# A vision tower with attention and a mixture of experts: scores from one projection, norms on ScalarE, a new order of TensorE's work per step

## The reference

```python
z = _layernorm(patches, ln1_g, ln1_b)
z = jnp.einsum('bnp,pe->bne', z, W_proj) + b_proj
z = _layernorm(z, ln2_g, ln2_b)
z = jnp.concatenate([cls, z], axis=1) + pos_emb
```

```python
q = jnp.einsum('blh,oh->blo', x, Wq) + bq
k = jnp.einsum('blh,oh->blo', x, Wk) + bk
v = jnp.einsum('blh,oh->blo', x, Wv) + bv
attn = jnp.einsum('blh,bmh->blm', q / hidden, k)
attn = jnp.where(eye[None, :, :], mask_value, attn)
return jnp.einsum('blm,bmh->blh', jax.nn.softmax(attn, axis=-1), v)
```

## Time and profile before

| | |
|---|---|
| median of 3 runs | 497.82 us (497.40 to 695.03) |
| the profiled execution | 497.69 us, of which span 496.0 us |
| PE busy | 376.4 us, 76% |
| DVE busy | 330.7 us, 67% |
| ACT busy | 210.0 us, 42% |
| POOL busy | 239.3 us, 48% |
| mean granted clock of TensorE | 0.861 of full |

### The profile page before, as it was taken

The page is one execution under the profiler, slowest core; times in us unless marked ns, Lnnn a source line. Parts: engine busy times, 40 slices in busy tenths (PEclk is TensorE's granted clock), DMA queues, the critical chain, the costliest instruction groups (busy, mean ns, idle before and its releaser), DMA issues.

```text
span 496.0 us, 7921 instructions
## 1 busy us (share of the span) xinstructions
PE 376.4 (76%) x2309; PEld 333.4 (67%) x2309; DVE 330.7 (67%) x863; ACT 210.0 (42%) x466; POOL 239.3 (48%) x399
## 2 busy tenths in 40 slices
PE   4585999999999998430136799999999999992000
PEld 1485999999999997330023599999999999991000
DVE  6463688777787866788881366667666676740692
ACT  4222445445445443272000256565656556532241
POOL 3254777777777755300002600835537274044395
PEclk9779899999999998755555699999999999997555
DMA  6423123323323201290002323656546475132833
GB/s 188 108 85 104 45 76 103 91 74 109 86 78 109 65 28 58 74 152 1 0 22 83 92 86 106 150 156 165 114 130 138 151 173 134 17 39 28 212 92 105
DMA packets 44676, 47.42 MB, mean 96 GB/s; under 512 B 11851, under 2 KB 36550, under 8 KB 44646
## 3 DMA queue, kind: packets, MB, share of 16 engines
q1 hardware_dynamic: 37940, 38.91, 28.0%
q0 software_dynamic: 5632, 7.36, 9.1%
q10 hardware_dynamic: 1074, 0.79, 0.6%
HBM read 32.38 MB, written 14.67 MB: 95 GB/s over the span
## 4 chain that ended last, share of the span: by engine, by line
PE 69%; DVE 12%; POOL 6%; DMA 4%; SPq 3%; issue 2%; ACT 1%; ACTq 0%; POOLq 0%; DVEq 0%
PE pz L796 16%; PE pall L809 16%; PE pall L703 9%; PE pall L672 8%; DVE wproj L1071 5%; PE pall L679 3%; SPq L423 3%; PE pall L769 2%; PE pall L713 2%; PE pz L659 2%; POOL stage L1354 2%; PE pall L720 1%; PE pall L821 1%; DMA stage<-in_x 1%; PE pall L692 1%
## 5 line engine op out<-in xcount | busy, mean ns | idle before, releaser
L1325 POOL DMA_INDIRECT y_rows<-rows,didx x32 | 50.7, 1585 | 95.2 <-ACT rows L606 87.9
L796 PE MATMUL pz<-halves 128*128 128x448 f32 x384 | 90.6, 373 | 2.1 <-DVE halves L1153 2.1
L809 PE MATMUL pall<-halves 128*128 128x448 f32 x384 | 89.9, 369 | 0.6 <-DVE halves L1148 0.6
L796 PEld LDWEIGHTS pz<-halves 128*128 128x128 f32 x384 | 73.7, 192 | 8.8 <-DVE halves L1153 2.5
L809 PEld LDWEIGHTS pall<-halves 128*128 128x128 f32 x384 | 70.9, 188 | 6.8 <-DVE halves L1148 1.0
L590 ACT ACTIVATE wproj<-pz,b1t 128x448 f32<-128x448 f32 x64 | 40.6, 635 | 73.8 <-PE pz L796 70.3
L1315 POOL DMA_INDIRECT rows<-x_rows,gidx x32 | 34.6, 1082 | 69.6 <-DVE gidx L1133 60.0
L703 PE MATMUL pall<-halves 128*112 128x256 f32 x396 | 55.1, 296 | 9.0 <-DVE halves L981 9.0
L1146 DVE CAST halves<-wproj 128x448 fp32r<-128x448 f32 x64 | 26.6, 416 | 50.0 <-ACT wproj L590 46.0
L703 PEld LDWEIGHTS pall<-halves 128*112 128x112 f32 x396 | 50.8, 186 | 9.9 <-DVE halves L981 7.4
L1223 POOL TENSOR_TENSOR rs<-rs,neghalf 112x1 f32<-112x1 f32 x88 | 50.1, 570 | 7.3
(11 more groups left out here) (211 smaller groups left out, 736.3 us busy)
## 6 DMA issues: line engine op xcount, KB each, us to landing
stage<-in_w SPq DMA_DIRECT2D x32, 512.0 KB, 4.2
stage<-in_x SPq DMA_DIRECT2D x64, 108.0 KB
x_rows<-x SPq DMA_DIRECT2D x22, 224.0 KB, 3.3
y_rows<-zero SPq DMA_DIRECT2D x22, 112.0 KB
stage<-y_rows SPq DMA_DIRECT2D x3, 448.0 KB, 5.4
out<-stage SPq DMA_DIRECT2D x7, 192.0 KB
scratch<-y_rows SPq DMA_DIRECT2D x2, 448.0 KB, 8.5
wproj<-in_w_proj ACTq DMA_DIRECT2D x1, 768.0 KB
```

What stands on the lines that cost most here:

```text
L796: m = nc.tensor.matmul(bank(k % 2)[:, 0:SLOTS], w[:, c, k * 128:(k + 1) * 128], xs[:, e % 2, c, :], start=(n == 0), stop=(n == 3 * EC - 1))
L809: m = nc.tensor.matmul(pall[:, 2 * (e % 2) + o, 0:SLOTS], w[:, k, o * 128:(o + 1) * 128], hs[:, k % 2, :], start=(k == 0 and n == 0), stop ...
L1325: pool.indirect_dma_start(y_rows, bass.IndirectOffsetOnAxis(ap=didx[:, k:k + 1], axis=0), y[:, e % 2, j, :], None, compute_op=ALU.add).the ...
```

## The change

**Scores from one projection.** The scores of a tile are x1 Wq' Wk x1' plus terms of the biases. Once, in steps 0 and 1, PE transposes both weights and multiplies them to one 256x256 matrix (`wqk`, kept in the place of `wq`), and makes the vectors that the biases give. Per tile there is then one projection t = x1 Wqk + tb (4 matmuls in place of 8), and the scores are t times x1's own transposes. The part of the bias that belongs to the key row rides as a 257th column of the value projection, from which DVE makes the exponential's offset (two small instructions, L1080 and L1083, in place of one).

**Norms on ScalarE.** ACT scales the projected row (L558), and writes x1 (L593) and x2 (L533); DVE did these three. DVE multiplies by the second norm's weights as it subtracts the mean (L1058). POOL now makes an offset as third small instruction for these two norms as well (`scaled`), and no longer multiplies. ACT also copies the logits (L562); the router's bias is added to all tiles at once later. POOL's addition of `lnb` moves into the experts, three tiles behind each gather.

**Four x slots**, loaded four tiles ahead, with one buffer for the normalised x in place of two.

The core of the diff:

```diff
-        wv = sb("wv", [128, EC, ED])
+        wqk = wq
+        wv = sb("wv", [128, EC, ED + 1])
...
-        xin = stage[0:P, 0:2 * PD].rearrange("p (s f) -> p s f", s=2)
-        xn = stage[0:P, 2 * PD:4 * PD].rearrange("p (s f) -> p s f", s=2)
+        xin = stage[0:P, 0:4 * PD].rearrange("p (s f) -> p s f", s=4)
+        xn = stage[0:P, 4 * PD:5 * PD]
...
+            for t in range(2, 4):
+                sp.wait_ge(s_xz, t + 1)
+                load_x(t, t)
+
+            def step(i, slot):
+                par = slot % 2
+                t = i + 4
                 if live(t):
                     need(sp, x_n, i + 1)
-                    load_x(t, par)
+                    load_x(t, slot)
...
+                t = i - 4
+                if live(t):
+                    plain(act, (x2T_ps, t - 1), (x2_out[par], 16 * (t // 2) if isinstance(t, int) else (t - par) * 8),
+                          (g_nb, t + 1))
+                    nc.scalar.activation(x2[:, par, :], tile_of(H, t), ACT.Identity, bias=rs[:, 3, 2:3],
+                                         scale=rs[:, 3, 1:2]).then_inc(x2_ok, 1)
+                t = i + 1
+                if live(t):
+                    high_x(t)
                 t = i - 3
+                if live(t):
+                    need(act, pT_ps, t + 1)
+                    need(act, o_ps, t)
+                    nc.scalar.copy(probT[:, :], bank(5)[0:P, 128:128 + P]).then_inc(pT_sb, 1)
...
+                t = i - 2
+                if live(t):
+                    need(act, t_ps, t + 1)
+                    need(act, s_ps, t)
+                    for c in range(EC):
+                        a = nc.scalar.activation(tT[:, c, :], bank(3)[:, c * P:(c + 1) * P], ACT.Identity,
+                                                 bias=tb[:, c:c + 1])
+                    a.then_inc(t_sb, 1)
+                t = i
+                if live(t):
+                    plain(act, (z_2, t + 1), (z_rs, t + 1))
+                    nc.scalar.activation(tile_of(H, t), z2[:, :], ACT.Copy, scale=rs[:, 1, 1:2]).then_inc(z_sc, 1)
+                t = i - 5
+                if live(t):
+                    plain(act, (l_ps, t + 1))
+                    nc.scalar.copy(LG[:, :, at(t)] if not isinstance(t, int) else LG[:, :, t:t + 1],
+                                   bank(2)[0:P, 256:256 + E].rearrange("p (e a) -> p e a", a=1)).then_inc(l_sb, 1)
...
+                t = i - 1
+                if live(t):
+                    need(act, x1T_ps, t + 1)
+                    need(act, s_ps, t - 1)
+                    nc.scalar.copy(x1T[:, odd, :], bank(6)[:, 0:EC * P]).then_inc(x1T_sb, 1)
+                t = i - 4
+                if live(t):
+                    need(act, x2T_ps, t + 1)
+                    need(act, l_ps, t)
+                    nc.scalar.copy(x2T[:, :], bank(3)[:, 256:256 + EC * P]).then_inc(x2T_sb, 1)
+                t = i - 2
                 if live(t):
                     need(act, s_nmx, t + 1)
                     need(act, pT_ps, t)
+                    need(act, g_h, t - 1)
                     nc.scalar.activation(prob[:, :], masked[:, :], ACT.Exp, bias=nmax[:, 0:1], scale=1.0 / ED,
+                                         accum_out=psumr[:, par:par + 1]).then_inc(p_ok, 1)
+                t = i + 2
+                if live(t):
+                    norm_x(t, (slot + 2) % 4)
                 t = i
                 if live(t):
+                    plain(act, (x1T_ps, t - 1), (h_nb, t + 1))
+                    nc.scalar.activation(x1[:, par, :], tile_of(H, t), ACT.Identity, bias=rs[:, 2, 2:3],
+                                         scale=rs[:, 2, 1:2]).then_inc(x1_ok, 1)
...
+                if isinstance(i, int) and i == 1:
+                    pe.wait_ge(c_ws, 2)
+                    pe.wait_ge(c_bq, 1)
+                    for o in range(EC):
+                        for c in range(EC):
+                            nc.tensor.matmul(bank(3)[:, o * ED:(o + 1) * ED], wqs[:, c, o * 128:(o + 1) * 128],
+                                             wks[:, c, :], start=(c == 0), stop=(c == EC - 1))
+                    for o in range(EC):
+                        for k, w in enumerate((wks, wqs)):
+                            for c in range(EC):
+                                nc.tensor.matmul(bank(4)[:, k * EC + o:k * EC + o + 1], w[:, c, o * 128:(o + 1) * 128],
+                                                 bqk[:, k * EC + c:k * EC + c + 1], start=(c == 0), stop=(c == EC - 1))
+                    for c in range(EC):
+                        m = nc.tensor.matmul(bank(4)[0:P, 2 * EC:2 * EC + 1], bqrep[:, c, :], bqk[:, EC + c:EC + c + 1],
+                                             start=(c == 0), stop=(c == EC - 1))
+                    m.then_inc(c_qk, 1)
                 t = i - 2
                 if live(t):
+                    if isinstance(t, int) and t == 0:
+                        pe.wait_ge(c_tv, 4)
+                    need(pe, x1T_sb, t + 1)
+                    need(pe, t_sb, t)
+                    need(pe, x2T_sb, t - 2)
+                    xt_ = x1T[:, par, :].rearrange("p (c r) -> p c r", c=EC)
+                    for o in range(EC):
+                        for c in range(EC):
+                            m = nc.tensor.matmul(bank(3)[:, o * P:(o + 1) * P], wqk[:, c, o * 128:(o + 1) * 128],
+                                                 xt_[:, c, :], start=(c == 0), stop=(c == EC - 1))
+                    m.then_inc(t_ps, 1)
+                t = i - 5
+                if live(t):
+                    need(pe, x2T_sb, t + 1)
+                    need(pe, l_sb, t)
+                    need(pe, z_2, i + 1 if not isinstance(i, int) else min(i + 1, TILES))
                     for c in range(EC):
+                        m = nc.tensor.matmul(bank(2)[0:P, 256:256 + E], x2T[:, c * P:(c + 1) * P], rw[:, c, :],
                                              start=(c == 0), stop=(c == EC - 1))
+                    m.then_inc(l_ps, 1)
...
+                t = i - 2
+                if live(t):
+                    need(pe, t_sb, t + 1)
+                    need(pe, s_msk, t)
+                    need(pe, pT_sb, t)
+                    for c in range(EC):
+                        m = nc.tensor.matmul(bank(5)[0:P, 0:P], tT[:, c, :], xt_[:, c, :],
+                                             start=(c == 0), stop=(c == EC - 1))
+                    m.then_inc(s_ps, 1)
...
+                    need(dve, z_ps, t + 1)
+                    need(dve, z_2, t)
+                    V_.bn_stats(zstat[:, :], bank(2)[0:P, 0:ED]).then_inc(z_st, 1)
+                    plain(dve, (z_st, t + 1), (z_rs0, t))
+                    V_.bn_aggr(zmv[:, :], zstat[:, :]).then_inc(z_mv, 1)
                     if isinstance(t, int) and t == 0:
+                        dve.wait_ge(c_g, N_G)
+                        V_.tensor_tensor(posb[:, :], posb[:, :], posadd[:, :], ALU.add).then_inc(c_dve, 1)
+                    plain(dve, (z_mv, t + 1), (z_sc, t))
+                    V_.scalar_tensor_tensor(z2[:, :], bank(2)[0:P, 0:ED], zmv[:, 0:1], g2m[:, :],
+                                            ALU.subtract, ALU.mult).then_inc(z_2, 1)
...
+                    V_.tensor_scalar(nm0[:, :], smax[:, :], v[:, par, ED:ED + 1], -1.0 / ED, ALU.add, ALU.mult)\
+                        .then_inc(s_nm0, 1)
+                    need(dve, s_nm0, t + 1)
+                    V_.scalar_tensor_tensor(nmax[:, :], v[:, par, ED:ED + 1], 1.0 / ED, nm0[:, :],
+                                            ALU.mult, ALU.add).then_inc(s_nmx, 1)
...
+            def scaled(slot, mv, ready, n, mid, done, nb):
+
+                rstd(slot, mv, ready, n, mid, done)
+                plain(pool, (done, n))
+                G.tensor_scalar(rs[:, slot, 2:3], mv[:, 0:1], rs[:, slot, 1:2], -1.0, ALU.mult, ALU.mult).then_inc(nb, 1)
+
...
+                    need(pool, z_sc, t)
+                    rstd(1, zmv, z_mv, t + 1, z_rs0, z_rs)
                     if isinstance(t, int) and t == 0:
                         pool.wait_ge(c_dve, 3)
+                    need(pool, z_sc, t + 1)
                     G.tensor_tensor(tile_of(H, t), tile_of(H, t), posb[:, :], ALU.add).then_inc(h_ok, 1)
                 if isinstance(i, int) and 2 <= i < 5:
                     (masks_table, live_table, index_table)[i - 2]()
                 t = i
                 if live(t):
+                    need(pool, x1_ok, t)
+                    scaled(2, hmv, h_mv, t + 1, h_rs0, h_rs, h_nb)
+                t = i + 3
+                if live(t):
+                    scale_x(t)
+                t = i - 3
+                if live(t):
+                    need(pool, x2_ok, t)
+                    scaled(3, gmv, g_mv, t + 1, g_rs0, g_rs, g_nb)
...
+                for t in range(3 * e, min(3 * e + 3, TILES)):
+                    G.tensor_tensor(H[:, t, :], H[:, t, :], lnb[:, :], ALU.add).then_inc(hb, 1)
                 scatter(e)
...
```

(19 more changed lines are left out.)

385 lines of the change are left out of this document (147 added, 238 removed).

## The result

The change makes the kernel slower: 519.98 us median (4 runs, 518.08 to 521.93) against 497.61 us (4 runs), ratio 1.045, 95% interval 1.0422 to 1.0479. One of the four runs of before, at 695.03 us, was a slow one and is not counted in the ratio. The forecast was 505 with 489 to 518, so the time lies outside the range, on the slow side.

What follows compares the result with a forecast made beforehand. PE, busy 20.00 of 20 us, was taken to bound the tile stage's 7.52 us step. 497.7 - 7 (first steps) + 12.5 (loop) + 2 (drain) = 505.2, so 505 us, range 489 to 518.

Steps and rivals of the forecast that it cites:

- A ring of one step: Tile stage: a loop of waits through DVE, POOL, ACT, POOL and DVE sets the step, whatever PE does.
- Its size, 8.65: Tile stage in the hardware loop: DVE 3.85, POOL 1.55 and 0.93, ACT 2.32 sum to 8.65 us per step.
- the branch through t and the scores: Tile stage: t, scores on PE, mask and exponential's offset meet DVE's statistics of H at nearly the same time; not summed.
- Rival 3, the clock: Tile stage: PE's idle time takes the clock down, half speed adds 4.8 to 9.6 us, 510 to 515 us; chance 0.19.
- The loop's gaps: Tile stage: dependent gaps of 0.17 to 0.24 us inside the hardware loop, 0.04 outside; step 8.65 inside, 7.5 outside.
- Rival 1: Tile stage: hardware-loop waits cost only 0.04 us as outside, step 7.5, the 12.5 go, 493 us; chance 0.14.
- Rival 2, PE at 6.63: Tile stage: no loop of waits binds, PE sets the step at 6.63 us, kernel 479 us; chance 0.09.
- The 12.5 for tiles 6 to 21: Tile stage, 15 steps between these products: 12.5 us longer, from 12 steps at 8.65 and 3 at 7.5.
- the 13.4: Tile stage, tiles 6 to 21: 126.3 against 112.9 us, +13.4, before allowing for ACT's wait at 0.04.
- First steps, -7: Start to product of tile 6: x wait -4.3, second product -2.5, POOL's factor -3, new costs; -7 us, bounds -10 and -3.
- Drain, +2: Past the last product: one more POOL instruction and hand-over, about 0.5 for each of four tiles; +2 us, bounds 0 and +4.
- The additions in the experts, 0 with +3 as bound: Experts: 22 additions of `lnb` fit POOL's idle time between gather and scatter; 0, up to +3 if they hold DVE's casts.

Runs made afterwards that it cites:

- the filled kernel: Changed kernel plus four useless matmuls on TensorE ahead of the logits, where it is idle in the loop: 520.44 us, ratio 1.0458 to the kernel before.
- e3_unrolled: Changed kernel with the 22 steps of the tile stage written out on all five engines, no hardware loop: 504.30 us, ratio 1.0121 to the kernel before.
- e10_before_x4: Kernel before with only the four slots for x: 493.60 us, ratio 0.9894.

## Why the prediction was wrong, step by step

- **A ring of one step would replace PE's bound: right.** Members and waits are as forecast, PE is idle ahead of the logits, and it took 9 us to take x2 out.
- **Its size, 8.65: too small, the step that failed.** Measured 9.26 in the turn shown: DVE 3.75 and 0.54 where I had 3.85 with the hand-over, POOL 1.54 for 1.55 and 0.91 for 0.93, ACT 2.52 for 2.32. ACT's wait was 0.27, not 0.17. Its x2 is 0.60 and occupies 0.51, not 0.41; the row it was taken from scaled `stage`, not a tile of H. On DVE 0.14 are small differences. The other 0.3 is the branch through t and the scores: I wrote that it met DVE "at nearly the same time" and did not add it up. At full clock the loop's step is 9.19 (the filled kernel), +0.54 x 12 = 6.5 us.
- **Rival 3, the clock, came on top.** I had made it an alternative of 0.19, priced at 4.8 to 9.6. By the filled kernel it cost 0.37 x 12 = 4.5 us (2.4 to 6.5 over the spread of the loop). In 72 to 74 PE was busy 0.47 of 2 us, and by 76 the clock stood at 0.50 (PE, windows of 2 us):

```profile
72.00:74.00 2.00, 0.47 (x5) 1.00 0.00 0
74.00:76.00 2.00, 1.68 (x10) 0.96 0.00 0
76.00:78.00 2.00, 1.69 (x8) 0.50 0.87 201
```

  With a ring above 8.65, PE's idle time grows too, so I take the two errors for linked, which no run shows by itself. I had treated them as cases side by side and had no case for both: together they are 11.0 us, and with the experts' 5.4 they leave the range.
- **The loop's gaps: right.** 1.13 per step was forecast (8.65 against 7.5), about 1.1 measured at full clock (9.19 against 8.06). Rival 1 is refuted: written out, the same order is 15.7 us faster. Dependent instructions of DVE stand 0.17 apart in the loop, 0.03 written out (L1090 to L1092 of `e3_unrolled`). The Trainium skill's rule of rival 1 (VectorE: DVE Perf Modes, section "The DRAIN you can't avoid"), that a semaphore between them costs nothing extra, is near the measured gap only for the code written out.
- **Rival 2, PE at 6.63:** refuted for the new order, true of the old one written out (6.71 with PE 89.84 of 90 us busy).
- **The 12.5 for tiles 6 to 21** was 24.7: 11.0 from 12 loop steps at 9.56, 0.4 from the other three (22.9 for 22.5), and 0.9 that I had taken off the 13.4 for a cheaper wait on ACT.
- **First steps, -7: too careful,** measured -10.5, just beyond my bound of -10. The wait for x alone was worth 4.4 in `e10_before_x4` (forecast 4.3). Tile by tile, the products of tiles 1 to 6 start 3.3, 3.9, 7.0, 12.6, 11.5 and 10.5 us earlier: -3.9 where I had -2.5 and +1 for the weights, then -3.1 for POOL's factor (forecast 3), then -5.7 where x had been late, and +2.1 in the last two, whose steps are 8.67 and 8.57, so the ring binds there already. The products of tile 6 in the kernels with this head start at 59.8 to 61.6, so terms of 1 us are within the spread. My other bound was a slip: only the wait for x gained, with all that comes, is -4.3 + 2.8 = -1.5, not -3.
- **Drain, +2:** +3.3, inside 0 to +4.
- **The additions in the experts, 0 with +3 as bound: failed.** I covered them by POOL's idle time and gave their hold on DVE's casts only a bound of +3; they cost 5.4. One kernel in the old order shows the same, +7.2 in that stretch.

Together: 497.7 - 10.5 + 24.7 + 3.3 + 0.2 + 5.4 = 520.8. The profiled execution took 521.16: 0.3 of the difference lies outside the span, the rest is rounding.

## What to carry to other kernels

When one engine is full, look for the ring that stands below it before you take work off it: here 0.89 us of PE per step could be won only as far as 7.35 in the hardware loop, and a new order with ACT's wait in the ring lost 1.7 (9.19 at full clock). In a ring, add up every branch that meets at its end, take each duration from the same operands, and write the steps out before judging an order, since gaps of 0.2 us cost nothing under a full engine and everything in a ring. Cover for an engine's work is not only its own idle time but also what its neighbour does meanwhile: in this kernel GpSimd's additions cost nothing beside VectorE's long compare, and they cost time beside its two-input instructions and its casts, though a cast has one input.

## What the runs showed of the hardware

- Back-to-back additions on GpSimd hold two-input instructions of VectorE: 0.21 became up to 0.65, 0.15 once 4.96, while a one-input reduction (0.24) and the compare (2.78) kept their times. Casts of 448 columns have one input and still went from 422 to 511 ns on average, and the additions themselves from 725 to 1023 ns. The Trainium skill (SBUF, section "SBUF: two separate sides") says that the two engines share one pair of ports as an exclusive lock: of a VectorE instruction with two SBUF inputs and a GpSimd one that reads SBUF, whichever starts first has it for its whole length, and the other waits. The trace agrees for the 0.65; the 4.96 is more than one instruction's wait.
- The same order of instructions took 9.19 us a step in the hardware loop (with four idle-time matmuls, clock 0.99) and 8.06 written out (clock 1.00).
- TensorE's clock fell to half in the changed kernel's loop (0.89 on average over 120 us, PE busy 100.39), stayed full written out (1.00, 106.44 busy) and nearly so with four idle-time matmuls (0.99, 106.25 busy). Products that ran while it was down lasted 3.4 to 4.4 us instead of 2.48.
